# A two-layer block on one core: the output projection of the second attention from 32-bit floats to pairs of 16-bit floats

## The reference, cut to what matters

```python
    # second layer; xn is the normed input, 16 heads of 64 numbers, INNER = 1024
    out = jnp.einsum('bhij,bhjd->bhid', probs, v)          # softmax attention
    out = out.transpose(0, 2, 1, 3).reshape(b, n, INNER)
    attn = out @ w_out + b_out                             # [2048,1024] @ [1024,128]
    ...
    h = jax.nn.silu(_tlin(x, w1_w, w1_s)) * _tlin(x, w2_w, w2_s)      # 128 -> 512
    h = jax.nn.gelu(_tlin(h, h1_w, h1_s), approximate=False)          # 512 -> 512
    h = jax.nn.gelu(_tlin(h, h2_w, h2_s), approximate=False)          # 512 -> 512
    ffn = _tlin(h, w3_w, w3_s)                                        # 512 -> 128
    return x + attn + ffn
```

## Time and profile before

| | us |
|---|---|
| three runs | 3351.94, 3344.41, 3352.87 (median 3351.94) |
| the profiled execution | 3346.46 |
| its span, first to last instruction | 3344.7 |
| second hidden layer of part 3, last chunk's gelu starts | 3283.75 |
| last instruction of DVE starts | 3341.67 |

### The profile page before, as it was taken

One profiled execution on the slowest core, in us unless ns is written; L12 is line 12 of the kernel. 1 busy time (PEld: TensorE's weight loads), 2 busy tenths in 40 slices (PEclk: granted clock), 3 DMA queues, 4 the chain that ended last, 5 costly groups with the idle time before them and its releaser, 6 DMA issues. The chain is left out here.

```text
span 3344.7 us, 58506 instructions
## 1 busy us (share of the span) xinstructions
PE 2978.6 (89%) x19523; PEld 1261.6 (38%) x19523; DVE 2775.2 (83%) x4212; ACT 2989.8 (89%) x2783; POOL 2504.1 (75%) x1645
## 2 busy tenths in 40 slices
PE   6888888888888888888888796999999999999899
PEld 4222222212221222122211342566656665666548
DVE  7889999999999999999999896877777787778341
ACT  3999999999999999999999684799999999999832
POOL 5888888888888888888868363688688877887650
PEclk9797778877887788778877897999999999999999
DMA  2000000000000000000000264000110011001100
GB/s 71 12 8 8 5 2 7 7 7 0 7 7 7 0 7 7 7 0 7 7 10 1 68 214 115 27 27 27 43 35 27 27 27 51 27 27 27 35 9 14
DMA packets 59509, 85.23 MB, mean 25 GB/s; under 512 B 10064, under 2 KB 45904, under 8 KB 58960
## 3 DMA queue, kind: packets, MB, share of 16 engines
q1 hardware_dynamic: 59344, 82.93, 8.6%
HBM read 52.31 MB, written 30.54 MB: 25 GB/s over the span
## 5 line engine op out<-in xcount | busy, mean ns | idle before, releaser
L1266 POOL TENSOR_TENSOR lo<-pr,hi 128x1024 f16<-128x1024 f32 x384 | 813.0, 2154 | 217.1 <-ACT hi L1445 215.0
L1326 DVE TENSOR_REDUCE mx<-mx_ps 128x1 f32<-128x512 f32 x1024 | 664.1, 686 | 195.3 <-PE mx_ps L1488 190.7
L1461 ACT ACTIVATE pr<-s_ps 128x1024 f32<-128x1024 f32 x512 | 529.1, 1033 | 111.6 <-PE s_ps L1519 105.4
L1445 ACT ACTIVATE hi<-pr 128x1024 f16<-128x1024 f32 x512 | 545.3, 1065 | 0.0
L722 ACT ACTIVATE wt<-wt 128x2048 f32<-128x2048 f32 x256 | 485.2, 1896 | 0.5
L713 ACT ACTIVATE wt<-wt,theta_bias 128x2048 f32<-128x2048 f32 (+2 forms) x160 | 482.3, 3015 | 3.0 <-DVE wt L563 2.5
L501 POOL TENSOR_TENSOR wt<-base,wt 128x1024 f32<-128x1024 f32 x192 | 455.3, 2371 | 16.1
L501 POOL TENSOR_TENSOR wt<-vb,wt 128x1024 f32<-128x1024 f32 x192 | 454.9, 2369 | 16.0
L1538 PE MATMUL pv_ps<-vh,hi 128*128 128x129 f16 x4096 | 425.2, 220 | 11.3 <-POOL lo L1266 5.7
L1538 PE MATMUL pv_ps<-vh,lo 128*128 128x65 f16 x4096 | 411.2, 193 | 0.0
L1488 PE MATMUL mx_ps<-ka,qa 128*128 128x512 f16 x1024 | 360.0, 387 | 54.5 <-DMA ka<-qk 28.4
(11 more groups left out here) (210 smaller groups left out, 5021.7 us busy)
## 6 DMA issues: line engine op xcount, KB each, us to landing
qk<-stg SPq DMA_DIRECT2D x6, 2048.0 KB, 10.8
vh<-v SPq DMA_DIRECT2D x16, 520.0 KB, 3.4
qa<-qk SPq DMA_DIRECT2D x16, 512.0 KB, 3.5
ka<-qk SPq DMA_DIRECT2D x32, 256.0 KB, 4.9
v<-v_st SPq DMA_DIRECT2D x3, 2080.0 KB, 7.9
qst<-parts_dram SPq DMA_DIRECT2D x144, 32.0 KB
kst<-parts_dram SPq DMA_DIRECT2D x144, 32.0 KB
qk<-stg SPq DMA_DIRECT2D x4, 1024.0 KB, 7.9
```

The source lines that it names most:

```text
L1266: eng.tensor_tensor(lo[:, i % NHL, :, :], pr_slot(i), hi[:, i % NHL, :, :], ALU.subtract).then_inc(lo_done, 1)
L1326: eng.tensor_reduce(mx4[:, q // NCH, q % NCH:q % NCH + 1], mx_ps[:, q % 2, :], AX.X, ALU.max)\
L1445: eng.activation(hi[:, i % NHL, :, :], pr_slot(i), ACT.Copy).then_inc(hi_done, 1)
L1461: eng.activation(pr_slot(i), s_ps[:, i % 2, :, :], ACT.Exp, scale=SM).then_inc(exp_done, 1)
```

## The change

It splits both operands of the attention's output product into two 16-bit floats.

- DVE writes the quotients no longer in place but into two buffers of 128x1024 (`quot`, in the storage of `h2`). Quotient k waits, from the third on, for POOL's subtraction of k-2.
- ACT rounds each quotient to its high half (`attn_high`), one instruction of 128x1024 after each gelu of the second hidden layer. It also rounds the output weights, scaled by 256, once (`wo_high`).
- POOL subtracts for the low half (`attn_low`), 16 times 128x1024, after the subtractions of part 2. It also makes a 16-bit identity.
- DVE makes the low half of the weights once, ahead of the quotients.
- `turn(k)` transposes eight high and eight low blocks in 16 bits. Each ACT copy to `aT` moves 128x1024 numbers of 16 bits.
- The product takes 24 matmuls in 16 bits. DVE multiplies by 1/256 where it adds `psO`.

```diff
                 def turn(k):
-                    eng.wait_ge(divided, k + 1)
-                    for b in range(2):
+                    for a, half_ready in enumerate((attn_high, attn_low)):
+                        eng.wait_ge(half_ready, k + 1)
                         if k >= 1:
-                            eng.wait_ge(aT_ready, 2 * (k - 1) + b + 1)
-                        for j in range(4):
-                            mm = eng.transpose(psU[:, b, j * P:(j + 1) * P],
-                                               attn1[:, k, (4 * b + j) * P:(4 * b + j + 1) * P], ident[:, :])
+                            eng.wait_ge(aT_ready, 2 * (k - 1) + a + 1)
+                        for j in range(MO):
+                            mm = eng.transpose(psU_h[:, a, j, :], attn_hl[:, k, a, j * P:(j + 1) * P], ident_16[:, :])
                         mm.then_inc(turned, 1)
+                eng.wait_ge(ident_ready, 1)
+                eng.wait_ge(wo_split, 1)
                 turn(0)
...
                     for j in range(MO):
-                        mm = eng.matmul(psO[:, k % 2, 0:D], aT[:, k % 2, j, :], wo[:, j, :],
-                                        start=(j == 0), stop=(j == MO - 1))
+                        for a, wa in TERMS:
+                            mm = eng.matmul(psO[:, k % 2, 0:D], aT_hl[:, k % 2, a, j, :], wo_hl[:, wa, j, :],
+                                            start=(j == 0 and a + wa == 0), stop=(j == MO - 1 and a == 1))
                     mm.then_inc(out_ps, 1)
...
             @block.scalar
+                eng.wait_ge(loaded, 16 * 4)
+                eng.activation(wo_hl[:, 0, :, :], wo[:, :, :], ACT.Copy, scale=WOS).then_inc(wo_high, 1)
                 for k in range(NM):
                     n_, m = k // M1, k % M1
                     eng.wait_ge(hid_ps, NM + k + 1)
                     eng.activation(ha[:, m, n_ * BANK:(n_ + 1) * BANK], psH[:, k % 2, :], ACT.Gelu,
                                    scale=sc[:, 3, m:m + 1]).then_inc(hid_ready, 1)
+                    eng.wait_ge(divided, k + 1)
+                    eng.activation(attn_hl[:, k, 0, :], quot[:, k % 2, :], ACT.Copy).then_inc(attn_high, 1)
                 for k in range(NT):
...
-                        eng.activation(aT[:, k % 2, 4 * b:4 * b + 4, :],
-                                       psU[:, b, :].rearrange("p (j t) -> p j t", j=4), ACT.Copy)\
-                           .then_inc(aT_ready, 1)
+                        eng.activation(aT_hl[:, k % 2, a, :, :], psU_h[:, a, :, :], ACT.Copy).then_inc(aT_ready, 1)
...
             @block.gpsimd
+                eng.tensor_copy(ident_16[:, :], ident[:, :]).then_inc(ident_ready, 1)
+                for k in range(NT):
+                    eng.wait_ge(attn_high, k + 1)
+                    eng.tensor_tensor(attn_hl[:, k, 1, :], quot[:, k % 2, :], attn_hl[:, k, 0, :],
+                                      ALU.subtract).then_inc(attn_low, 1)
...
             @block.vector
+                eng.wait_ge(wo_high, 1)
+                eng.scalar_tensor_tensor(out=wo_hl[:, 1, :, :], in0=wo[:, :, :], scalar=WOS, in1=wo_hl[:, 0, :, :],
+                                         op0=ALU.mult, op1=ALU.subtract).then_inc(wo_split, 1)
+                eng.wait_ge(h_split, 2)
                 for k in range(NT):
-                    by_head = attn1[:, k, :].rearrange("p (h e) -> p h e", h=H)
-                    eng.tensor_tensor(by_head, by_head, rden[:, k, :].unsqueeze(2).to_broadcast([P, H, HD1]),
+                    if k >= 2:
+                        eng.wait_ge(attn_low, k - 1)
+                    eng.tensor_tensor(quot[:, k % 2, :].rearrange("p (h e) -> p h e", h=H),
+                                      attn1[:, k, :].rearrange("p (h e) -> p h e", h=H),
+                                      rden[:, k, :].unsqueeze(2).to_broadcast([P, H, HD1]),
                                       ALU.mult).then_inc(divided, 1)
```

More of the change, by code:

```diff
@@ L58 @@
 NHL = 8
+WOS = 256.0
 def stage_project0(nc, io, sb):
@@ L1639, in stage_output @@
         turned, aT_ready, divided = sem("turned_e"), sem("aT_ready"), sem("divided")
+        quot = h2[:, :, :].rearrange("p k o -> p (k o)").rearrange("p (a e) -> p a e", a=2)
+        attn_hl = attn1[:, :, :].rearrange("p n e -> p (n e)").bitcast(F16).rearrange("p (n a e) -> p n a e", n=NT, a=2)
+        aT_hl = aT[:, :, :, :].rearrange("p a j t -> p (a j t)").bitcast(F16)\
+                              .rearrange("p (s a j t) -> p s a j t", s=2, a=2, j=MO)
+        psU_h = psU[:, :, :].rearrange("p b c -> p (b c)").bitcast(F16).rearrange("p (b j t) -> p b j t", b=2, j=MO)
+        wo_hl, ident_16 = t("wo_hl", [P, 2, MO, D], F16), t("ident_16", [P, P], F16)
+        attn_high, attn_low = sem("attn_high"), sem("attn_low")
+        ident_ready, wo_high, wo_split = sem("ident_ready_e"), sem("wo_high"), sem("wo_split")
         loaded, weights_loaded = sem("loaded_e"), sb["weights2_loaded"]
@@ L1753, in _ @@
                                    scale=sc[:, 3, m:m + 1]).then_inc(hid_ready, 1)
+                    eng.wait_ge(divided, k + 1)
+                    eng.activation(attn_hl[:, k, 0, :], quot[:, k % 2, :], ACT.Copy).then_inc(attn_high, 1)
                 for k in range(NT):
-                    for b in range(2):
-                        eng.wait_ge(turned, 2 * k + b + 1)
+                    for a in range(2):
+                        eng.wait_ge(turned, 2 * k + a + 1)
                         if k >= 2:
                             eng.wait_ge(out_ps, k - 1)
-                        eng.activation(aT[:, k % 2, 4 * b:4 * b + 4, :],
-                                       psU[:, b, :].rearrange("p (j t) -> p j t", j=4), ACT.Copy)\
-                           .then_inc(aT_ready, 1)
+                        eng.activation(aT_hl[:, k % 2, a, :, :], psU_h[:, a, :, :], ACT.Copy).then_inc(aT_ready, 1)
             @block.gpsimd
@@ L1814, in _ @@
                     eng.wait_ge(out_ps, k + 1)
-                    eng.tensor_tensor(y[:, k, :], y[:, k, :], psO[:, k % 2, 0:D], ALU.add).then_inc(y_sum, 1)
+                    eng.scalar_tensor_tensor(out=y[:, k, :], in0=psO[:, k % 2, 0:D], scalar=1.0 / WOS, in1=y[:, k, :],
+                                             op0=ALU.mult, op1=ALU.add).then_inc(y_sum, 1)
                     eng.wait_ge(y_sum, k + 1)
```

## The result

| | us |
|---|---|
| before, 14 runs | 3349.52 (3344.41 to 3352.87) |
| changed, 14 runs | 3354.33 (3350.11 to 3361.80) |
| ratio, 95% interval | 1.0018 (1.0010 to 1.0026), +3.3 to +8.7 us |
| profiled executions, before and changed | 3346.46 and 3352.70 |

What follows compares the result with a forecast made beforehand. TensorE was taken as the bound. Output -5.9, bare copy +0.5, waits among quotients, roundings and subtractions +11.0, low clock +1.7 gave +7.3, rounded to +7: 3357 us from base 3350.4, 8-in-10 range 3346 to 3368.

Steps and rivals of the forecast that it cites:

- What bounds the kernel: In the last 141 us, TensorE almost alone: hidden layers' matmuls 82.89 us, then the output at 3.55 us a tile.
- The output's gain: Output on TensorE: 57 ns per 16-bit step, 3.17 us a tile for 3.55, -5.9 us (-4.6 to -7.8) in all.
- rival of pacing weight loads: Rival: weight loads of 99 ns pace the 16-bit output matmuls; about +33 us in all, 3364 to 3384; chance 0.06.
- The ring: Second hidden layer: quotient, rounding, subtraction wait in a circle, DVE and POOL excluding each other; turn(1) +11.0 us (+8.3 to +11.7).
- from the fifth on: Second hidden layer: TensorE stalls 1.3 us in every second chunk, starting with the fifth.
- The clock: Behind five idle microseconds ahead of turn(1), TensorE at 1.2 GHz for 3.4 us of work: +1.7 us (0.5 to 3.5).
- bare copy: At the output's start, turn(1)'s second half waits for the second, longer ACT copy to `aT`: +0.5 us.
- The sum: Whole kernel: -5.9 + 0.5 + 11.0 + 1.7 = +7.3 us, rounded to +7; bounds +1.5 and +11.
- base of 3350.4: Assumed time of the kernel before, set between mean and median of earlier runs, to which +7 was added for 3357.
- The output's gain stands: Rival: DVE and POOL overlap in the second hidden layer, nothing else lost; -3.9 us, 3345 to 3348; chance 0.12.
- costlier ring: Rival: worse order of turns in second hidden layer, or 1.2 GHz over several output tiles; 3361 to 3368; chance 0.12.

Runs made afterwards that it cites:

- output alone: Changed kernel without ACT's separate rounding and POOL's subtraction, quotients' low half left out; second hidden layer's first to last output matmul 93.9 us (before 99.1), whole-time ratio 0.9971.
- ring alone: Changed kernel's quotients, roundings and subtractions, but 32-bit transposes, copies and products as before; second hidden layer's first to last output matmul 111.2 us (before 99.1), whole-time ratio 1.0029.
- reciprocals in PSUM: Changed kernel, but quotients read the reciprocals from PSUM, leaving one SBUF input; second hidden layer's first to last output matmul 96.6 us (before 99.1), whole-time ratio 0.9983.
- DVE subtracts: Changed kernel with the 16 subtractions on DVE instead of POOL; second hidden layer's first to last output matmul 94.9 us (before 99.1), whole-time ratio 0.9975.
- four buffers: Changed kernel with four quotient buffers instead of two; second hidden layer's first to last output matmul 101.4 us (before 99.1), whole-time ratio to before 0.9999.
- early tiles: Changed kernel with PSUM reciprocals, weights' split and four tiles moved into first hidden layer, network output reordered; second hidden layer's first to last output matmul 93.1 us, ratio to before 0.9972.

## Why the prediction was right

**What bounds the kernel** held: the output lay on TensorE alone, and both the gain and the loss came out on the chain.

**The output's gain.** Foreseen 57 ns a step and 3.17 us a tile, measured 0.89 / 16 = 56 ns for a transpose and 1.34 / 24 = 56 ns for a matmul, but L1725 took 0.95 us and not 0.89: 3.18 in all. Behind turn(1) the tiles gained 6.0 us (output alone), where -5.9 was forecast. The rival of pacing weight loads is gone. The Trainium skill's 81 ns for a pair of load and matmul at 128 columns (TensorE: Matmul & The Clock Gate, Back-to-back issue gap) does not hold here; the measurement decides.

**The ring** was the term that decided, and it came nearly as foreseen. A round took 6.46 us (6.5). The first weights' low half, quotient 0 and rounding 0 ended at 3245.5, 3246.7 and 3247.8 (3245.8, 3247.0, 3248.1, with the whole stage 0.3 us earlier in this profile). The last subtraction ended at 3297.3 (3297.9). TensorE's chunks began 1.28 us late every second time (1.3; the rows show 1.11, since the record of 24 matmuls lasts 5.35 us and not 5.18), it idled 4.76 us (about 5), and turn(1) stood 53.8 us into the stretch against 43.0: +10.8 (+11.0). Two details were off. The gaps began at the eighth chunk and not "from the fifth on"; the five gaps that fit the forecast end of the layer came. And the forecast's round waits for both quotients (1.14 + 0.05 us behind the first), while the chain goes from the first quotient over its rounding to POOL (1.07 + 0.09). The second quotient ended at 3260.76 and the rounding at 3260.73, so both paths have the same length here by chance of their sizes; with a longer rounding the round would have been forecast too short. That the cause is the exclusion and not the ring's shape was inference then. Three runs show it now: one operand's place removes the loss, more buffers remove less than half, and taking POOL away removes it too. The Trainium skill's rule (SBUF — State Buffer, Who interferes with whom) is that a DVE instruction with two SBUF inputs contends with a POOL one that reads SBUF, and that one with a single SBUF input does not, outside what the page calls "2-port perf modes". The trace agrees for the quotients: 3.13 us with two SBUF inputs, 1.22 with one. One SBUF input alone is not enough, as the CAST of 0.43 us shows that lasted 1.88 beside a subtraction.

**The clock** fell as foreseen, to 0.50 (1.2 GHz) for 3.4 us from 3295.7, and was over-sized: 1.2 us instead of 1.7. The 0.5 us for the bare copy and the clock's cost were counted one beside the other, and they overlap: at half speed the transposes take as long as the copy. Without the clock the bare copy costs 0.4, and in the ring alone, which has the short copies, the clock cost the full 1.7.

**The sum.** +7.3 foreseen. In the same terms the runs give -6.0 + 0.4 + 10.8 + 1.2 = +6.4, the stretch +6.5, the ratio +3.3 to +8.7. The 0.8 too much are the clock's 0.5 and smaller terms. The base of 3350.4 was 0.9 above the later median of 3349.5. The rest of the 2.7 us between 3357 and 3354.3 is the sum's excess and a difference of the medians, 4.8 us, that lies below the stretch's 6.5 and inside the interval.

**The rivals.** "The output's gain stands" did not happen, but the kernel with reciprocals in PSUM is that case: -2.6 us in the stretch with a low clock, and -4.2 in the kernel where DVE subtracts and the clock stayed up; -3.9 was its forecast. The costlier ring did not come.

## What to carry to other kernels

Work that is moved to idle engines has to be priced as a chain, with what each instruction excludes, not by busy shares: DVE and POOL each stood idle for over 50 of 83 us, and yet each of 16 pairs ran one after the other. Look in the trace of before for a place where the two engines' instructions of these kinds meet; two such places carried this forecast. Where they exclude each other, change the place of one operand of a two-input instruction or the engine before adding buffers. It should also help to keep work that other engines wait for out of the queue behind such a wait; this was not tried by itself.

## What the runs showed of the hardware that I had not expected

- The same idle stretch of 1.83 us on TensorE was followed by a granted clock of 0.50 (1.2 GHz) in one kernel and of 1.00 (2.4 GHz) in another. Windows of the two, reciprocals in PSUM first, which was idle until 3285.56, then the kernel where DVE subtracts, which was idle until 3291.16:

```profile
3286.80:3290.20 3.40, 3.40 (x28) 3.34 (x25) 0.29 (x1) 1.46 (x2) 0.00 (x0) 0.50 0.00 0
```

```profile
3290.00:3294.00 4.00, 2.53 (x34) 2.41 (x35) 1.52 (x2) 3.76 (x5) 0.00 (x0) 1.00 0.00 0
```

  From turn(1)'s start to turn(2)'s it is 5.28 us in the first and 3.65 in the second, and by these 1.6 us their stretches differ. Behind 0.89 us (output alone) it stayed at 1.00, behind 5.97 us (four buffers) it was 0.50. Each is one profiled execution, so whether the kernel or the execution decides at 1.83 us is open.
- Four 32-bit products (L1725) between 16-bit transposes and 16-bit products take 0.95 us in all kernels with the 16-bit output, and 0.89 between 32-bit ones. What makes the 0.06 us was not tried.
- A small instruction pays in full: POOL's 128x128 copy of the identity, which meets the weights' split on DVE, was recorded at 1.29 us. In the kernel with early tiles, beside a quotient with one operand in PSUM, it was recorded at 0.29.
